# Cross-attention and mixture-of-experts kernel: the inverse sums of the softmax applied to the probabilities ahead of their transposes, by GpSimd and VectorE, in place of a transposed copy of them

## The chip, the core and the metric

The kernel runs on one core of one Trainium2 chip. A core has a matrix engine (TensorE, PE in the rows), which writes to eight banks of PSUM, and three engines for elementwise work: VectorE (DVE), ScalarE (ACT) and GpSimd (POOL). They share a memory of 128 partitions, SBUF. Each engine works off its own instructions in their order and waits for others on semaphores. The metric is the time of one execution on the device in microseconds (us); less is better.

## What is computed

32 sequences of 112 tokens with 512 channels go through one layer: causal cross-attention with 16 heads of 32 channels, then a mixture of eight experts and a shared expert. The change is in the attention.

```python
def _L0_xattn_ref(q, latent_kv, Wq, Wkv_expand, Wout):
    B, S, H, NH, L = (2, 512, 512, 16, 128)
    HD = H // NH
    qp = q @ Wq.T
    kv = latent_kv @ Wkv_expand.T
    k, v = jnp.split(kv, 2, axis=-1)
    ...
    scores = jnp.einsum('bhqd,bhkd->bhqk', qh, kh) * inv_sqrt_d
    scores = jnp.where(causal, scores, jnp.finfo(scores.dtype).min)
    attn = jax.nn.softmax(scores, axis=-1)
    out = jnp.einsum('bhqk,bhkd->bhqd', attn, vh)
    out = out.transpose(0, 2, 1, 3).reshape(b, sq, H)
    return out @ Wout.T

x = x + _L0_xattn_ref(_layernorm(x, axis=-1), ctx_512, L0_xattn_Wq, L0_xattn_Wkv_expand, L0_xattn_Wout)
x = x + _L0_ffn_ref(_layernorm(x, axis=-1), ...)
```

## The kernel before, in words

The program has three phases: attention and routing (phase A), the experts (63 tiles of 128 tokens), and the shared expert with the sum of all. Phase A runs over eight groups g of four batches j, so batch t is 4g + j; two further rounds of the loop drain the pipeline and begin the shared expert (`hidden0`, `project0`). One round for one batch is a *step*. All order is written by hand: each engine has a function for its step, and the engines meet on semaphores. The four upper PSUM banks are handed round by the table `TURNS`; the four lower ones hold the scores.

**TensorE's step t** (`step`, then `next_front`): value product of batch t (L823), mask (L937) and scores (L947) of batch t; 16 transposes of the *probabilities of batch t-1* (L956), four to a bank; four transposes of `rinv_wide` (L964); the products of probabilities and values, `outT`, of batch t-1 (L975); transposes of a normalised row block (L984, `normT`, batch t-3); output projection of batch t-2 (L823, `proj`); router (L1013); in the third step of a group two rank products (L914, L915); queries and keys of the next batches (L823). Large products are made of three, from a high and a low part of each operand (`_hi`, `_lo`).

**ScalarE's step**: `v_sb`; four copies `probsT` of the transposed probabilities out of PSUM (L1240); 16 exponentials of batch t with their row sums `rsum` (L1251), and after the eighth of them the copy `rinvT` (L1229); after the sixteenth `aT_hi` (L1262); then queries, keys and the next input's high part. `exp_done` counts halves of eight heads.

**VectorE's step**: `rinv` = 1/`rsum` of batch t-1 (L1685); twice the maximum over half of the scores and `minus_max` (L1692, L1694); statistics of the next input (L1580, L1583); `xn2T` (L1650); the low part of an input (L1605); `attnT` = `outT` times `rinvT` (L1717); `x1`, the residual sum of batch t-2 (L1726); `logits`; statistics of `x1`; `aT_lo` (L1738); and then `choices`: in the groups from the third on (g = 2 to 6) a chain of small instructions that chooses experts for the group before, 10 in the first step (j = 0), 11 lines in the second (13 instructions) and 6 in the fourth (`place`; not in g = 6). The third step has three others (`route_z`). In g = 7 the choices stand behind `minus_max`.

**GpSimd's step**: `rinv_wide` (L1486), `rinv` of batch t-1 copied 32 times for each head; indirect DMAs of token lists (L1439, two a step); in the first and the third step of a group the split of the context (L1430, L1432); `scaled_root` (L1419, L1421); `rows` for batch t-2: twice a small instruction and `xn` (L1474), which `normT` of the next step waits for. In g = 7 and later `rows` stands ahead of the indirect DMAs.

The whole scores bank of batch t may be written only when batch t-1's exponentials are done (L937 waits for `exp_done`).

## Time and profile before

| | us |
|---|---|
| median of 3 runs | 1514.03 (1512.74 to 1515.2) |
| the profiled execution, its own time | 1509.76 |
| span of its profile | 1508.0 |
| PE busy in the span | 1482.2 (98%) |
| DVE, ACT, POOL busy | 857.5, 653.0, 592.4 |
| granted TensorE clock | 0.999 of full speed |

A profile page first gives the busy time of each engine over the whole span, then the span in 40 slices of 37.7 us with a digit for the busy tenths of each, then the chain of work that ended last. Phase A fills the first eleven slices or so. Timelines list instructions in order of time, with an idle time and who ended it in brackets; the chain of waits lists at each moment what the end of the kernel hung on.

### The profile page before, as it was taken

The page shows a single profiled execution, that of the slowest core. Times are in us where ns is not written, and L with a number is a line of the kernel's source. Part 1 is how long each engine was busy: PE and PEld are TensorE (multiplying, and loading weights), DVE is VectorE, ACT ScalarE, POOL GpSimd, SP SyncE. Part 2 cuts the span into 40 slices and gives each one's busy share as a digit, 9 for nine tenths or more (in the row PEclk, how much of TensorE's full clock was granted, in tenths as well). Part 3 has the DMA queues.
Part 4 walks back from the last instruction along what each step waited for, and adds up shares of the span by engine and source line. Part 5 has one row for each costly group of instructions (what it writes and reads, how often), then busy time and mean ns, then how long its engine had stood idle before and what let it go on. Part 6 is the DMA issues. An engine that isn't in the chain of part 4 may idle for free.

```text
span 1508.0 us, 28385 instructions
## 1 busy us (share of the span) xinstructions
PE 1482.2 (98%) x10074; PEld 1261.6 (84%) x10074; DVE 857.5 (57%) x1458; ACT 653.0 (43%) x1836; POOL 592.4 (39%) x505
## 2 busy tenths in 40 slices
PE   8999999999989999999999999999999999999999
PEld 7788888888778899999999999887888888888887
DVE  5566777777756587786877867455223232223322
ACT  6999998999843322332332333332112121211211
POOL 3333455555552387595775864102101102011010
PEclk9999999999999999999999999999999999999999
DMA  6244434434365689877868765553303122030110
GB/s 225 87 118 118 118 112 117 117 95 121 82 139 111 179 309 340 275 246 264 284 232 275 279 215 175 176 202 88 95 15 112 28 73 61 6 112 28 59 54 28
DMA packets 102905, 217.44 MB, mean 144 GB/s; under 512 B 43696, under 2 KB 48816, under 8 KB 98064
## 3 DMA queue, kind: packets, MB, share of 16 engines
q1 hardware_dynamic: 91184, 184.71, 37.8%
q0 software_dynamic: 11616, 31.35, 7.2%
q8 instruction: 63, 1.03, 0.3%
q14 instruction: 42, 0.34, 0.1%
HBM read 168.86 MB, written 47.17 MB: 143 GB/s over the span
## 4 chain that ended last, share of the span: by engine, by line
PE 86%; ACT 7%; DVE 3%; issue 3%; POOL 1%; DMA 0%; DVEq 0%; POOLq 0%; ACTq 0%
PE psum L823 61%; PE psum L1146 11%; ACT probs L1251 5%; PE psum L956 2%; PE psum L906 2%; PE psum L1048 2%; PE psum L947 2%; PE psum L1072 1%; PE psum L975 1%; PE psum L1013 1%; ACT probsT L1240 1%; PE psum L964 1%; PE psum L984 1%; PE psum L937 1%; PE psum L837 0%
## 5 line engine op out<-in xcount | busy, mean ns | idle before, releaser
L1568 POOL DMA_INDIRECT routed<-expert_out_dram,slot_b x56 | 56.7, 1012 | 478.5 <-DVE slot_b L2016 328.0
L1251 ACT ACTIVATE probs<-psum,minus_max,rs 112x112 f32<-112x112 f32 x512 | 222.2, 503 | 3.6 <-DVE minus_max L1694 3.4
L2034 DVE TENSOR_TENSOR h_s<-psum,silu_s 128x512 f32<-128x512 f32 x66 | 45.7, 692 | 298.3 <-PE psum L823 290.0
L823 PE MATMUL psum<-nT_hi,ws_hi 128*128 128x512 f32 x528 | 208.8, 395 | 3.4 <-DVE nT_lo L1957 3.1
L823 PE MATMUL psum<-nT_lo,ws_hi 128*128 128x512 f32 x528 | 208.6, 395 | 0.0
L823 PE MATMUL psum<-nT_hi,ws_lo 128*128 128x512 f32 x528 | 208.6, 395 | 0.0
L1540 POOL DMA_INDIRECT xg<-normed_dram,tile_ids x63 | 149.9, 2380 | 36.1 <-DMA tile_ids<-lists_dram 17.4
L823 PE MATMUL psum<-wj_hi,gT_hi 128*128 128x352 f32 x504 | 162.8, 323 | 0.0
L823 PE MATMUL psum<-wj_hi,gT_lo 128*128 128x352 f32 x504 | 162.3, 322 | 0.0
L823 PE MATMUL psum<-wj_lo,gT_hi 128*128 128x352 f32 x504 | 161.8, 321 | 0.0
L1371 ACT ACTIVATE silu_s<-psum 128x512 f32<-128x512 f32 x66 | 39.4, 597 | 242.9 <-PE psum L823 242.9
L1251 ACT ACTIVATION_READ_ACCUMULATOR probs<-psum,minus_max,rs 112x1 f32 x512 | 135.7, 265 | 0.0
L1374 ACT ACTIVATE hs_hi<-h_s 128x512 fp32r<-128x512 f32 x66 | 41.7, 632 | 199.0 <-DVE h_s L2034 196.0
L1942 DVE TENSOR_TENSOR wj_lo<-wj_raw,wj_hi 128x2816 fp32r<-128x2816 f32 x35 | 121.7, 3476 | 9.4 <-POOL wj_hi L1523 7.2
L823 PEld LDWEIGHTS psum<-nT_hi,ws_hi 128*128 128x128 f32 x528 | 99.2, 188 | 27.6 <-DVE nT_lo L1957 3.5
L1523 POOL TENSOR_SCALAR wj_hi<-wj_raw 128x2816 fp32r<-128x2816 f32 x34 | 87.4, 2570 | 83.1 <-issue 75.8
L823 PEld LDWEIGHTS psum<-nT_hi,ws_lo 128*128 128x128 f32 x528 | 99.2, 188 | 23.8
L823 PEld LDWEIGHTS psum<-nT_lo,ws_hi 128*128 128x128 f32 x528 | 99.2, 188 | 23.3
L1146 PE MATMUL psum<-ws_lo,hs_hi 128*128 128x512 f32 x264 | 103.4, 392 | 0.0
L1146 PE MATMUL psum<-ws_hi,hs_hi 128*128 128x512 f32 x264 | 103.3, 391 | 0.0
L1146 PE MATMUL psum<-ws_hi,hs_lo 128*128 128x512 f32 x264 | 102.9, 390 | 0.0
L823 PEld LDWEIGHTS psum<-wj_lo,gT_hi 128*128 128x128 f32 x504 | 94.9, 188 | 2.6
(256 smaller groups left out, 3446.2 us busy)
## 6 DMA issues: line engine op xcount, KB each, us to landing
wj_raw<-in_w_experts SPq DMA_DIRECT2D x35, 1408.0 KB
wj_raw<-in_w_experts SPq DMA_DIRECT2D x35, 768.0 KB
wj_raw<-in_w_shared SPq DMA_DIRECT2D x22, 768.0 KB, 4.4
expert_out_dram<-y_c SPq DMA_DIRECT2D x63, 256.0 KB
base<-x_dram SPq DMA_DIRECT2D x8, 1024.0 KB, 5.9
xT_raw<-in_xT SPq DMA_DIRECT2D x32, 224.0 KB
x_in<-in_x SPq DMA_DIRECT2D x32, 224.0 KB
x_res<-in_x SPq DMA_DIRECT2D x32, 224.0 KB, 3.1
```

Of the source, the lines that this page charges most:

```text
L823: mm = pe.matmul(out_ap, u, v, start=(n == 0), stop=(n == last))
L906: mm = pe.matmul(bank(j), u, v, start=(c == 0 and q == 0), stop=(c == SC - 1 and q == 2))
L947: mm = pe.matmul(psum[0:SEQ, r, m * SEQ:(m + 1) * SEQ], qT[g % 2][rows, m, tok], kT[rows, m, tok], start=False, stop=(m == KC - 1))
L1146: mm = pe.matmul(bank(j), u, v, start=(i == 0 and q == 0), stop=(i == SC - 1 and q == 2))
L1251: done = act.activation(probs[:, j % 2, 4 * r + m, :], psum[0:SEQ, r, m * SEQ:(m + 1) * SEQ], ACT.Exp, bias=minus_max[:, r, m:m + 1], scal ...
L1371: act.activation(silu_s[:, :], bank(b), ACT.Silu).then_inc(emptied_b[b], 1)
L1374: act.activation(hs_hi[:, i % 2, :], h_s[:, :], ACT.Copy).then_inc(S["hs_hi_made"], 1)
L1523: pool.tensor_scalar(wj_hi[b][:, FC_COLS], wj_raws[b][:, FC_COLS], 1.0, 0.0, ALU.mult, ALU.add).then_inc(S["wc_hi_made"], 1)
L1540: pool.indirect_dma_start(out=xg[b][:, :], out_offset=None, in_=normed_dram, in_offset=bass.IndirectOffsetOnAxis(ap=tile_ids[:, k % ROUND: ...
L1568: pool.indirect_dma_start(out=routed[:, b % 2, c, :], out_offset=None, in_=expert_out_dram, in_offset=bass.IndirectOffsetOnAxis(ap=slot_b[ ...
L1942: dve.tensor_tensor(wj_lo[b][:, FC_COLS], wj_raws[b][:, FC_COLS], wj_hi[b][:, FC_COLS].bitcast(F32), ALU.subtract).then_inc(S["wc_split"], 1)
L2034: dve.tensor_tensor(h_s[:, :], bank(b), silu_s[:, :], ALU.mult).then_inc(emptied_b[b], 1)
```

## The change

The probabilities are multiplied by the inverse sums before they are transposed. GpSimd multiplies heads 0 to 7 of a batch in place as soon as their eight exponentials are done, VectorE heads 8 to 15 when all are. With that `rinv_wide`, its transposes, the copy `rinvT` and the product `attnT` go; `aT_hi` and `aT_lo` are made directly from the bank of `outT`, and ScalarE makes `aT_hi` after the fourth exponential. The order of the sums follows that of the probabilities. The freed SBUF goes into a gap, so that what follows keeps its place.

```diff
@@ TURNS
-    TURNS += [((_j, "sumT", 0), 1, 5), ((_j, "outT", 0), 1, 7),
+    TURNS += [((_j, "outT", 0), 1, 7),
@@ TensorE, step
-                    pe.wait_ge(S["exp_done"], 2 * t)
+                    pe.wait_ge(S["first_normed"], t)
+                    pe.wait_ge(S["normed"], t)
                     for i in range(4):
                         b = take(g, j, "probsT", i)
...
-                if there(g, j, 1):
-
-                    pe.wait_ge(S["rinv_spread"], t)
-                    b = take(g, j, "sumT")
-                    for m in range(KC):
-                        mm = pe.transpose(psum[:, b, m * SEQ:(m + 1) * SEQ], rinv_wide[:, 4 * m:4 * m + 4, :].rearrange("s h d -> s (h d)"),
-                                          ident[0:SEQ, 0:SEQ])
-                    mm.then_inc(filled[b], 1)
...
-                        pe.wait_ge(S["attnT_split"], t - 1)
+                        wait_emptied(pe, g, j - 1, "outT")
@@ ScalarE, body
+                    def attnT_high():
+                        if there(g, j, 3):
+                            wait_filled(act, g, j - 1, "proj")
+                        b = turns.bank("outT")
+                        wait_filled(act, g, j, "outT")
+                        act.activation(aT_hi[:, (j + 1) % 2, :, :].rearrange("p k s -> p (k s)"), bank(b, P, GT), ACT.Copy).then_inc(S["attnT_hi_made"], 1)
...
-                                                          accum_out=rsum[:, j % 2, 4 * m + r:4 * m + r + 1])
+                                                          accum_out=rsum[:, j % 2, 4 * r + m:4 * r + m + 1])
+                                if r == 0 and there(g, j, 1):
+                                    attnT_high()
                             done.then_inc(S["exp_done"], 1)
-                            if i == 0 and there(g, j, 1):
-                                rinv_to_rows()
@@ GpSimd, body
-                        pool.wait_ge(S["rinv_made"], t)
-                        settled(pool)
-                        pool.tensor_copy(rinv_wide[:, :, :], rinv[:, :].unsqueeze(2).to_broadcast([SEQ, HEADS, HD])).then_inc(S["rinv_spread"], 1)
...
                     if there(g, j, -1):
                         scaled_root(t + 1)
+                    if there(g, j, 0):
+                        pool.wait_ge(S["rinv_made"], 2 * t + 1)
+                        settled(pool)
+                        pool.tensor_tensor(probs[:, j % 2, 0:8, :], probs[:, j % 2, 0:8, :], rinv[:, 0:8].unsqueeze(2).to_broadcast([SEQ, HEADS // 2, SEQ]),
+                                           ALU.mult).then_inc(S["first_normed"], 1)
@@ VectorE
+            def normalise(t, i):
+                half, n = slice(8 * i, 8 * i + 8), 2 * t + i
+                dve.wait_ge(S["exp_done"], n + 1)
+                at_least(dve, S["normed"], t)
+                at_least(dve, S["first_normed"], t)
+                dve.reciprocal(rinv[:, half], rsum[:, t % 2, half]).then_inc(S["rinv_made"], 1)
+                if i == 0:
+                    return
+                dve.wait_ge(S["rinv_made"], n + 1)
+                dve.tensor_tensor(probs[:, t % 2, half, :], probs[:, t % 2, half, :], rinv[:, half].unsqueeze(2).to_broadcast([SEQ, HEADS // 2, SEQ]),
+                                  ALU.mult).then_inc(S["normed"], 1)
...
                 if there(g, j, 1):
-                    dve.reciprocal(rinv[:, :], rsum[:, (j + 1) % 2, :]).then_inc(S["rinv_made"], 1)
+                    normalise(t - 1, 1)
...
                     b = turns.bank("outT")
-                    dve.tensor_tensor(attnT[:, :], bank(b, P, GT), rinvT[:, :], ALU.mult).then_inc(emptied[b], 1)
+                    dve.wait_ge(S["attnT_hi_made"], t)
+                    hi = aT_hi[:, (j + 1) % 2, :, :].rearrange("p k s -> p (k s)")
+                    dve.tensor_tensor(aT_lo[:, (j + 1) % 2, :, :].rearrange("p k s -> p (k s)"), bank(b, P, GT),
+                                      hi.bitcast(F32), ALU.subtract).then_inc(emptied[b], 1)
...
-                if there(g, j, 1):
-
-                    dve.wait_ge(S["attnT_hi_made"], t)
...
+                if there(g, j, 0):
+                    normalise(t, 0)
                 if is_late(g, 0) or not is_late(g, 2) or (j < TB - 1 and not is_late(g)):
                     choices(g, j)
```

VectorE, end of a fourth step (j = 3) and begin of the next, before. `rt_eq` to `slots_i` are the six instructions of `place`, `rinv` to `minus_max` the next step's head:

```order
L1583 BN_AGGR mv<-stat 112x2
L1738 TENSOR_TENSOR aT_lo<-attnT,aT_hi 128x448
L1815 TENSOR_TENSOR rt_eq<-rt_rank,rt_one 112x32
L1816 TENSOR_REDUCE route<-rt_eq 112x4
L1817 CAST slots_i<-route 112x4
L1815 TENSOR_TENSOR rt_eq<-rt_rank,rt_one 112x32
L1816 TENSOR_REDUCE route<-rt_eq 112x4
L1817 CAST slots_i<-route 112x4
L1685 RECIPROCAL rinv<-rsum 112x16
L1692 TENSOR_REDUCE smax<-psum 112x8
```

The same place in the changed program:

```order
L1566 BN_AGGR mv<-stat 112x2
L1666 RECIPROCAL rinv<-rsum 112x8
L1802 TENSOR_TENSOR rt_eq<-rt_rank,rt_one 112x32
L1803 TENSOR_REDUCE route<-rt_eq 112x4
L1804 CAST slots_i<-route 112x4
L1802 TENSOR_TENSOR rt_eq<-rt_rank,rt_one 112x32
L1803 TENSOR_REDUCE route<-rt_eq 112x4
L1804 CAST slots_i<-route 112x4
L1666 RECIPROCAL rinv<-rsum 112x8
L1670 TENSOR_TENSOR probs<-probs,rinv 112x896
L1683 TENSOR_REDUCE smax<-psum 112x8
```

A first reciprocal now stands ahead of the choices, `aT_lo` has gone to the front of the step, and the multiplication of eight heads stands between the choices and the next maximum.

GpSimd, from `rows` of a fourth step to `scaled_root` in the next, before (`rs` and `xn` are `rows`, the last two `rs` are `scaled_root`):

```order
L1474 TENSOR_SCALAR xn<-x,mv,rs 112x512
L1486 COPY rinv_wide<-rinv 112x512
L1439 DMA lists_dram<-token_id,slots_i 28672x1 x2
L1419 TENSOR_SCALAR rs<-mv 112x1
L1421 TENSOR_TENSOR rs<-rs,neg_half 112x1
L1419 TENSOR_SCALAR rs<-mv 112x1
L1421 TENSOR_TENSOR rs<-rs,neg_half 112x1
```

and in the changed program:

```order
L1458 TENSOR_SCALAR xn<-x,mv,rs 112x512
L1423 DMA lists_dram<-token_id,slots_i 28672x1 x2
L1403 TENSOR_SCALAR rs<-mv 112x1
L1405 TENSOR_TENSOR rs<-rs,neg_half 112x1
L1483 TENSOR_TENSOR probs<-probs,rinv 112x896
L1403 TENSOR_SCALAR rs<-mv 112x1
L1405 TENSOR_TENSOR rs<-rs,neg_half 112x1
```

The copy at the head of the step is gone, and a multiplication of 896 columns stands between `scaled_root` and `rows`.

## Rows read from the trace of the kernel before

**Rows 1.** The page: busy time by engine, and ScalarE's busy tenths in 40 slices.
```profile
PE 1482.2 (98%) x10074; PEld 1261.6 (84%) x10074; DVE 857.5 (57%) x1458; ACT 653.0 (43%) x1836; POOL 592.4 (39%) x505
...
ACT  6999998999843322332332333332112121211211
```
**Rows 2.** Chain of waits, batch 7 of phase A: start us, us, engine and line.
```profile
110.31 1.68 PE psum L956 x16
...
111.99 0.57 PE psum L964 x4
...
116.78 0.70 PE psum L1013 x8
...
122.70 0.34 PE psum L956 x2
```
**Rows 3.** The same chain: the transposes L956 at the heads of groups 6 and 7.
```profile
326.44 1.68 PE psum L956 x16
...
377.84 0.54 PE psum L956 x4
```
**Rows 4.** Timeline of ScalarE, batch 7: start us, us, line, out<-in, shape, count.
```profile
110.87 1.84 ACT L1240 ACTIVATE probsT<-psum 112x448 f32<-112x448 f32 x4 [1.01 <-PE psum L956]
...
119.74 0.70 ACT L1262 ACTIVATE aT_hi<-attnT 128x448 fp32r<-128x448 f32 x1
```
**Rows 5.** Timeline of VectorE, batch 7.
```profile
117.19 0.68 DVE L1726 TENSOR_TENSOR x<-psum,x_res 112x512 f32<-112x512 f32 x1
...
118.76 0.18 DVE L1583 BATCH_NORM_AGGREGATE mv<-stat 112x2 f32<-112x6 f32 x1 [0.16 <-DVE stat L1580]
```
**Rows 6.** Timelines around a second step's choices: first, last, then VectorE's reciprocal and GpSimd's reply.
```profile
146.51 0.18 DVE L1798 SCALAR_TENSOR_TENSOR rt_rest<-rt_one,rt_p 112x32 f32<-112x32 f32 x1
...
149.09 0.17 DVE L1806 TENSOR_TENSOR chosen<-chosen,rt_pick 112x8 f32<-112x8 f32 x1
149.18 0.25 DVE L1685 RECIPROCAL rinv<-rsum 112x16 f32<-112x16 f32 x1
...
149.58 0.61 POOL L1486 COPY rinv_wide<-rinv 112x512 f32<-112x512 f32 x1 [2.15 <-issue]
```
**Rows 7.** Operands in SBUF alone: two by tile (ns min/median/max), one of a timeline.
```profile
L1459 POOL TENSOR_TENSOR n_lo<-xT_raw,n_hi x2: 1123/1123/1123, 9.8 to 10.9; 128x448 fp32r<-128x448 f32 x2
...
L1605 DVE TENSOR_TENSOR xT_lo<-xT_raw,xT_hi x16: 615/616/1082, 21.9 to 332.7; 128x448 fp32r<-128x448 f32 x16
...
13.12 1.22 DVE L1600 TENSOR_TENSOR wq_lo<-wj_raw,wq_hi 128x1024 fp32r<-128x1024 f32 x1 [1.13 <-ACT wq_hi L1169]
```
**Rows 8.** Timelines: VectorE and GpSimd at once, both reading SBUF, at three places.
```profile
543.46 2.92 POOL L1531 TENSOR_SCALAR wj_hi<-wj_raw 128x1536 fp32r<-128x1536 f32 x2
...
544.72 4.61 DVE L1942 TENSOR_TENSOR wj_lo<-wj_raw,wj_hi 128x2816 fp32r<-128x2816 f32 x1
...
23.92 0.92 POOL L1432 TENSOR_TENSOR ctx_lo<-ctx_in,ctx_hi 128x224 fp32r<-128x224 f32 x1
...
23.63 1.69 DVE L1605 TENSOR_TENSOR xT_lo<-xT_raw,xT_hi 128x448 fp32r<-128x448 f32 x2 [0.56 <-ACT xT_hi L1174]
...
145.35 2.08 POOL L1474 TENSOR_SCALAR xn<-x,mv,rs 112x512 f32<-112x512 f32 x1 [0.31 <-PE psum L823]
...
145.56 1.03 DVE L1738 TENSOR_TENSOR aT_lo<-attnT,aT_hi 128x448 fp32r<-128x448 f32 x1 [1.53 <-ACT aT_hi L1262]
```
**Rows 9.** Timelines: `place` and its cast beside `xn`.
```profile
222.17 2.08 POOL L1474 TENSOR_SCALAR xn<-x,mv,rs 112x512 f32<-112x512 f32 x1 [0.31 <-PE psum L823]
...
223.77 0.51 DVE L1817 CAST slots_i<-route 112x4 int32<-112x4 f32 x1
```
**Rows 10.** Chain of waits and timeline of TensorE: the transposes L956 of the last batches.
```profile
400.42 0.54 PE psum L956 x4
...
411.77 0.54 PE psum L956 x4
...
421.50 1.75 PE L956 MATMUL psum<-ident,probs 112*112 112x112 f32 x16 [1.53 <-ACT probs L1251]
```

36 lines of the change are left out of this document (5 added, 31 removed).

## The prediction

> **What bounds the kernel now.** I read the page first: PE is busy for 98% of the span, and ScalarE is dense only in the first eleven slices [rows 1], phase A, the one phase that the change touches. Then the chain of waits in a step of phase A without choices [rows 2]: it is all PE, and from one batch's transposes to the next takes 122.70 - 110.31 = 12.39 us. I call the start of these transposes R. In the groups with choices the chain leaves PE for VectorE and ScalarE; the mean group there takes (326.44 - 122.70) / 4 = 50.94 us [rows 2, 3], against 4 x 12.39 = 49.56 plus some 0.42 for the rank products. The last batches have no queries left and go at 411.77 - 400.42 = 11.35 [rows 10]. So the question is two-fold: how much shorter does PE's step get, and does anything new arrive later than PE at R?
>
> **PE's step.** The four transposes L964 go: 0.57 us on the chain [rows 2]. They also covered ScalarE's copies: these end at 110.87 + 1.84 = 112.71, R + 2.40 [rows 4]. `outT` would now start at R + 1.68 and reach the last quarter of its 32 products, after some 0.68, at R + 2.36: about 0.10 of waiting with the signal. PE's step becomes 12.39 - 0.57 + 0.10 = 11.92.
>
> **ScalarE.** `rinvT` goes and `aT_hi` takes its place, so the exponentials still end at 119.74, R + 9.43 [rows 4]. It gets 0.47 more idle time (the old `aT_hi`), which is worth nothing while PE is last.
>
> **VectorE until the first reciprocal.** `attnT` waited for `rinvT`; `aT_lo`, in its place, is done by some R + 5.3, ahead of `x1`, which now waits for PE's projection alone. That ended at 116.78, R + 6.47 [rows 2], now at R + 6.00, and with 0.15 for the signal `x1` starts at R + 6.15. From its start to the end of the statistics it is 118.94 - 117.19 = 1.75 [rows 5]: R + 7.90. The reciprocal of the first half ends at R + 8.10, and GpSimd answers a reciprocal after 149.58 - 149.43 = 0.15 [rows 6]: its multiplication starts at R + 8.25.
>
> **GpSimd's multiplication.** 448 columns of two SBUF operands took 1.12 us on GpSimd [rows 7], 224 took about 0.6 once let in [rows 8]; the slope is some 2.0 ns a column, so 896 take an estimated 2.03 us (bounds: twice 1.12 = 2.25; by `xn`, 2.08 for 512 columns, 3.64). It ends at R + 10.3; `rows` follows, 1.2 us of small work with its gaps and `xn` from about R + 11.5 to 13.6. `normT` needs it at R + 11.92 + 2.6: hidden, with 0.9 to spare. Indirect DMAs and `scaled_root` come after it and end some 6 us into the next step, ahead of the next reciprocal.
>
> **VectorE's multiplication.** 448 columns take 0.615, 1024 take 1.22 [rows 7]: 896 take about 1.09, and 0.2 for the reciprocal. In a step without choices it could start at R + 9.43 + 0.3 = 9.75 and end at 10.85, a full microsecond before PE wants it. But both engines would then read SBUF at once, which rows 8 show three times. `wj_lo` started while GpSimd worked until 543.46 + 2.92 = 546.38, and ended at 549.33, 2.95 later, its own whole length by the 1024-column row. The second of two `xT_lo` took 1.08 for 0.62 [rows 7] beside a `ctx_lo` of GpSimd, itself late by the first. Beside `xn`, whose 2.08 us outlast it, `aT_lo` took only 1.03: it was let in about 0.65 us after `xn` began. So a two-operand instruction of VectorE stands still while GpSimd reads; a GpSimd TENSOR_TENSOR reads to its end (one row of a short one), `xn` for 0.65 us. I take the first for the multiplication, since it is the same operation.
>
> The Trainium skill, in "SBUF — State Buffer", section "Who interferes with whom", calls this an exclusive lock: a VectorE instruction with two SBUF inputs and a GpSimd instruction that reads SBUF block each other for the whole instruction. The trace agrees for `wj_hi` and `ctx_lo`; `xn` was passed before its end. By the rule to the letter `xn` would also hold VectorE until R + 13.6, and the steps with choices would be some 1.5 us longer each than below; the rows decide against that.
>
> **Steps without choices.** VectorE's multiplication waits until R + 10.3, ends at 11.4, and with 0.1 for the signal is ready at 11.5. PE comes at 11.92. Hidden, by 0.4. Five such steps before R = 122.70: 5 x -0.47 = -2.35. The first three steps hang on ScalarE and on loads: 0.
>
> **Steps with choices.** Here the choices stand between the two reciprocals, in the middle of GpSimd's multiplication. They run at (149.26 - 146.51) / 13 = 0.21 each [rows 6].
> First step: two one-operand instructions until R + 8.5, then `rt_p` has two operands and waits until 10.3, ends 10.45; seven more, 1.5, and some 0.2 for `xn`'s reading: 12.2; reciprocal 12.4; multiplication 13.5 to 13.6; R' = 13.7.
> Second step: `rt_rest` slips in, `rt_eq` waits until 10.3; nine more, 2.1, and 0.3 for `xn`: 12.9; multiplication ends 14.2; R' = 14.3.
> Fourth step: the cast in `place` waits to the end of a GpSimd instruction even beside `xn`: 223.77 + 0.51 = 224.28, where `xn` ended at 224.25 [rows 9]. So it waits until 10.3; three more, 0.65; multiplication ends at 12.25; R' = 12.35.
> Third step: 11.92 + 0.42 for the ranks, and 0.06 if `rt_z` is caught: 12.4.
> Sum 52.75 against 50.94: +1.81 a group, four groups: +7.2. Group 6 has no `place`: 13.7 + 14.3 + 12.4 + 11.92 = 52.3 against 377.84 - 326.44 = 51.40: +0.9. Who waits in each case is PE, at the transposes; behind them all its work for the step. ScalarE waits in turn, and the maxima come after the multiplication but still 1 us ahead of ScalarE.
>
> **Last batches.** In group 7 the choices come early in the step and push `x1` to about R + 7.0, the first reciprocal to 8.95, GpSimd's multiplication to 9.1 to 11.1, just ahead of VectorE's (ready 9.75): that ends at 12.2, R' = 12.3 against 11.35, about +1.0, three times. Last batch: 421.50 - 411.77 = 9.73 from R to the last transposes [rows 10], which wait for nothing but exponentials; now 10.35 + 1.1 + 0.1 = 11.55, +1.8, less 0.8 for the L964 and its wait: +1.0. In the drain `aT_lo` leaves the stretch between statistics and choices: -0.5. Together +3.5.
>
> **Sum.** -2.35 + 7.2 + 0.9 + 3.5 = +9.25. The later phases are PE at full load behind phase A, and shift. The profiled execution took 1509.76, now 1519.0. It lies 4.3 under the median 1514.03; on the median's footing, which I forecast: 1523.3.
>
> **Rivals.**
> A short hold: the multiplication lets VectorE in after 0.65 us as `xn` does, or never stops it. Then the choices end at R + 10.6 to 11.2, R' is 12.0, 12.6, 12.34, 12.35: 49.3 a group, -1.65 x 4 = -6.6; group 6 -2.5; steps without choices -2.35; the last batches about 0: -11.4, time 1502.6. With no hold at all 48.2 to 48.5 a group and 1497. For it: `xn`, and that only one short row shows a TENSOR_TENSOR of GpSimd holding to its end. Against: `wj_hi` held for 2.6 us to its end. Chance 0.20.
> A slow multiplication: by `xn`'s rate 3.64 us, ending at R + 11.9. Then VectorE's multiplication ends at 13.0 even without choices, R' = 13.1, and every step with choices gains 1.6 more: 4 x 8.1 + 7 + 5 x 0.75 + 9.8 = +53, 1567. For it only that one of its operands is a repeated number; against: `rinv_wide` repeated the same one at 0.61 for 512 columns [rows 6]. It decides from 2.4 us on. Chance 0.05.
> Nothing in sum: VectorE wins the race at `rt_rest` and in group 7 in enough steps to bring +9 down to within 3. Chance 0.08, time about 1514.
> My forecast has 0.67, between 1515 and 1535: the 0.3 to 0.5 us by which the choices meet `xn`, or 0.2 more for the multiplication, move it by some 4 each.
>
> **How the numbers follow.** Range 1502 to 1535: the forecast with its bounds, the case of nothing, and the upper end of the short hold, about 0.82 together (0.64, 0.08 and half of the 0.20). A measurement tells 0.2%, 3 us, from no change. Slower: 0.67 + 0.05 = 0.72; within: 0.08; faster: 0.20.
>
> **What would show it.** R to R in a step without choices 11.9; first and second steps of a group 13.7 and 14.3 with PE idle before the transposes of the probabilities until VectorE's multiplication ends; `rt_p` in the first and the first `rt_eq` in the second step at some 1.8 us instead of 0.19; GpSimd's multiplication 2.0 us from R + 8.25. A short hold would show all choices at 0.2. Wrong would be the forecast if GpSimd came late to its multiplication, after VectorE's own, which would turn the waiting round.

## The result, and the profile of the changed kernel

| | before | changed |
|---|---|---|
| median | 1514.22 us (1512.74 to 1515.2, 4 runs) | 1523.13 us (1522.02 to 1524.24, 4 runs) |
| profiled execution, its span | 1509.76, 1508.0 | 1524.24, 1522.5 |
| granted clock, mean of that span | 0.999 | 0.992 |

The changed kernel is slower: ratio 1.007, with a 95% interval of 1.0057 to 1.0082 (the two medians alone give 1.006). The forecast was 1523.3.

The page of the changed kernel answers to [rows 1]. PE's work has shrunk by 2.8 us and VectorE's has grown by 40, GpSimd's by 44; the matrix engine is busy for 97% of a longer span.

```profile
PE 1479.4 (97%) x9946; PEld 1253.0 (82%) x9946; DVE 897.5 (59%) x1490; ACT 639.4 (42%) x1804; POOL 636.0 (42%) x505
```

As in the prediction, R is the start of the transposes of the probabilities (L954 now). I read the first of each batch from TensorE's timeline, for every kernel in the same way, and take the differences of four places: R(8), the begin of the groups with choices; R(28), their end; R(32), the last batch; and the span. The tables below use these columns.

| | R(8) | R(8) to R(28) | R(28) to R(32) | behind R(32) | span |
|---|---|---|---|---|---|
| before | 122.6 | 255.1 | 43.7 | 1086.5 | 1508.0 |
| changed | 120.6 | 264.4 | 50.1 | 1087.5 | 1522.5 |
| difference | -2.1 | +9.3 | +6.3 | +1.0 | +14.5 |

The program of the phases behind phase A is unchanged; what the +1.0 behind R(32) is made of stands in the part on the prediction. First the chain of waits in a step without choices, which answers to [rows 2]: start us, us, engine and line.

```profile
108.53 1.68 PE psum L954 x16
110.20 0.75 PE psum L965 x24
...
110.99 0.40 PE psum L965 x8
...
120.62 0.43 PE psum L954 x3
```

The L964 are gone, and the step takes 12.09 where it took 12.39. The product `outT` (L965) starts at once and stops after 24 of its 32 parts, because ScalarE's last copy of `probsT` is not there.

Then the first step with choices. The timeline of VectorE (start us, us, line, operation, out<-in, idle before) and below it GpSimd's and TensorE's of the same stretch; compare [rows 6]:

```profile
129.18 1.61 DVE L1769 TENSOR_TENSOR rt_p<-rt_e,rt_r 112x32 f32<-112x32 f32 x1
...
132.15 0.66 DVE L1782 TENSOR_TENSOR rt_one<-prefer,route 112x32 f32<-112x32 f32 x1
132.84 0.20 DVE L1666 RECIPROCAL rinv<-rsum 112x8 f32<-112x8 f32 x1
133.07 1.09 DVE L1670 TENSOR_TENSOR probs<-probs,rinv 112x896 f32<-112x896 f32 x1
...
129.07 1.69 POOL L1483 TENSOR_TENSOR probs<-probs,rinv 112x896 f32<-112x896 f32 x1 [3.74 <-DVE rinv L1666]
...
132.00 2.08 POOL L1458 TENSOR_SCALAR xn<-x,mv,rs 112x512 f32<-112x512 f32 x1 [0.31 <-POOL rs L1405]
...
134.27 1.72 PE L954 MATMUL psum<-ident,probs 112*112 112x112 f32 x16 [1.52 <-issue]
...
142.88 1.60 DVE L1779 TENSOR_TENSOR rt_eq<-rt_rest,route 112x32 f32<-112x32 f32 x1
...
142.75 1.68 POOL L1483 TENSOR_TENSOR probs<-probs,rinv 112x896 f32<-112x896 f32 x1 [4.11 <-DVE rinv L1666]
```

`rt_p`, an instruction of 32 columns, stands for 1.61 us, until 130.79, and GpSimd's multiplication ends at 130.76. Everything behind it is late: the choices, the second reciprocal, VectorE's multiplication, which ends at 134.16. TensorE has idled for 1.52 us and starts at 134.27. In the second step it is `rt_eq` that stands (1.60 us, beside the multiplication from 142.75, the last two lines). The steps of this first group take 13.7, 13.8, 12.5 and 12.6.

Last, the end of phase A, by windows of the span (us, busy us of each engine, PEclk, DMA share, GB/s) and in TensorE's timeline; before, the clock was 1.00 in all of it, and the transposes took 1.75 [rows 10]:

```profile
395.00:400.00 5.00, 5.00 (x89) 3.93 (x88) 4.08 (x4) 2.37 (x6) 4.22 (x4) 0.70 0.47 134
...
420.00:425.00 5.00, 3.56 (x48) 3.41 (x40) 4.77 (x8) 1.44 (x3) 4.37 (x4) 0.69 0.30 88
...
422.15 3.21 PE L954 MATMUL psum<-ident,probs 112*112 112x112 f32 x16 [1.44 <-issue]
...
435.04 3.21 PE L954 MATMUL psum<-ident,probs 112*112 112x112 f32 x16 [4.63 <-issue]
```

After idle times of 1.44 and 4.63 us the clock stands at its lower level, 1.2 GHz, and the same 16 transposes take 3.21 us.

### The profile page after: what moved, and what is told of

Read it like the earlier page. It is cut to its first block, busy times and chain, and to the rows that moved or that the text cites. A ratio compares the mean times of both kernels' runs of the same rounds, so it can differ in the third digit from the quotient of the medians.

```text
span 1522.5 us, 28070 instructions
## 1 busy us (share of the span) xinstructions
PE 1479.4 (97%) x9946; PEld 1253.0 (82%) x9946; DVE 897.5 (59%) x1490; ACT 639.4 (42%) x1804; POOL 636.0 (42%) x505
## 4 chain that ended last, share of the span: by engine, by line
PE 91%; ACT 4%; issue 2%; DVE 2%; POOL 0%; DMA 0%; another core or an unknown queue 0%; POOLq 0%; DVEq 0%; ACTq 0%
PE psum L820 63%; PE psum L1136 11%; PE psum L954 3%; ACT probs L1241 3%; PE psum L944 2%; PE psum L903 2%; PE psum L965 2%; PE psum L1038 2%; PE psum L1062 1%; PE psum L1003 1%; PE psum L974 1%; PE psum L934 1%; ACT probsT L1230 1%; PE psum L834 0%; DMA routed<-expert_out_dram,slot_b 0%
## 5 line engine op out<-in xcount | busy, mean ns | idle before, releaser
L1523 POOL DMA_INDIRECT xg<-normed_dram,tile_ids x63 | 150.1, 2382 | 35.6 <-DMA tile_ids<-lists_dram 12.8
```

What stands on the lines that cost most here:

```text
L1523: pool.indirect_dma_start(out=xg[b][:, :], out_offset=None, in_=normed_dram, in_offset=bass.IndirectOffsetOnAxis(ap=tile_ids[:, k % ROUND: ...
```

## The experiments

My theory was the hold (H): VectorE's small instructions stand while GpSimd multiplies, and that pushes VectorE's own multiplication past the transposes. The rivals: that it is only the place and length of VectorE's new work (P), and that the loss is at the end, with the clock (C, K).

Each set of experiments ran beside the kernel before, whose median was 1512.59, 1512.07, 1512.32 and 1513.19 us there; the ratios below are against these. The changed kernel itself was not run again, so a difference from its 1523.13 is sure to some 2 us only.

### GpSimd multiplies one column

```diff
-    pool.tensor_tensor(probs[:, j % 2, 0:8, :], probs[:, j % 2, 0:8, :], rinv[:, 0:8]..., ALU.mult)
+    pool.tensor_tensor(probs[:, j % 2, 0, 0:1], probs[:, j % 2, 0, 0:1], rinv[:, 0:1], ALU.mult)
```

> The changed kernel, but GpSimd multiplies one column of the probabilities instead of 896: heads 0 to 7 are left without their inverse sums. Everything else, the waits and signals too, is unchanged. Theory H (hold): VectorE's instructions with two SBUF operands, and its cast, stand still while GpSimd's multiplication reads, and that is what pushes VectorE's own multiplication past the transposes. Then rt_p in a group's first step and the first rt_eq in its second go back from 1.6 us to 0.19; the choices end at some R + 10.6 (one of them beside xn, +0.5), R to R' in the first step is 12.2 instead of 13.65 and in the second 12.8 instead of 13.8, the fourth 12.1; a group takes 49.6 instead of 52.9, five of them -16, and the last batches give back 1 to 3: 1504 to 1507. Rival P (place): what costs is only that a reciprocal and a multiplication of 1.09 us stand behind the choices; then the group keeps 52 to 53 us and the time stays within 3 of the changed kernel's 1523. Rival C (the end): the loss is the clock and the drain at the last batches; then the groups keep their 52.9 and only the stretch behind R(28) gets shorter, by some 4: 1519.

Measured 1511.15 (1506.05 to 1514.73, 10 runs), 0.9992 of before (0.9979 to 1.0006). VectorE's timeline:

```profile
129.84 0.19 DVE L1769 TENSOR_TENSOR rt_p<-rt_e,rt_r 112x32 f32<-112x32 f32 x1
...
131.39 0.55 DVE L1782 TENSOR_TENSOR rt_one<-prefer,route 112x32 f32<-112x32 f32 x1
```

| | R(8) | R(8) to R(28) | R(28) to R(32) | span |
|---|---|---|---|---|
| one column | 121.2 | 248.9 | 50.9 | 1507.5 |

`rt_p` is back at 0.19, and five groups take 248.9 us, 15.5 less than in the changed kernel; 16 were expected. Against a run of the same 28 batches without the stands described in the last section (261.7 us, the kernel with neither multiplication in the last four batches, below) it is 12.8. Of the choices only the instruction beside `xn` is still long. P and C both fall for the groups: VectorE's multiplication is still there, and the groups gain. But the last four steps did not get shorter at all, where 1 to 3 were expected; so the time is 1511, not 1504 to 1507. One of these steps took 15.4, and in it ScalarE stood for 4.41 us, for which the trace names no releaser; GpSimd's indirect DMAs ran in the second half of it.

### GpSimd writes zeros instead

```diff
-    pool.tensor_tensor(probs..., ALU.mult).then_inc(S["first_normed"], 1)
+    pool.memset(gap_a[0:SEQ, 0:1664], 0.0).then_inc(S["first_normed"], 1)
```

> The changed kernel, but GpSimd writes 1664 columns of a spare tile with zeros (448 columns took it 0.46 us, so about 1.7) in the place and with the waits and signals of its multiplication: it is as long busy, but reads no SBUF. Heads 0 to 7 are left without their inverse sums. Theory H in its form 'it is GpSimd's reading': VectorE goes through, rt_p 0.19, the same time as with the multiplication of one column, 1504 to 1507, except that rows and xn come 1.7 later and xn holds one instruction, as in the changed kernel. Rival W: any work of GpSimd on SBUF, writing too, holds VectorE's two-operand instructions; then rt_p still takes 1.6, a group 52.9, the time 1523. Rival P as before: 1523 without a long rt_p.

Measured 1513.58 (1511.54 to 1516.71, 10 runs), 1.0007 of before (0.9998 to 1.0017). VectorE's timeline and GpSimd's:

```profile
129.32 0.19 DVE L1768 TENSOR_TENSOR rt_p<-rt_e,rt_r 112x32 f32<-112x32 f32 x1
129.54 1.15 DVE L1769 TENSOR_SCALAR rt_g<-rt_ge 112x4 f32<-112x4 f32 x1
...
129.18 1.49 POOL L1483 MEMSET gap_a<- 112x1664 f32 x1 [3.24 <-DVE rinv L1665]
```

Neither form of the expectation holds as it stood. `rt_p`, with two operands, passes beside the write; the next instruction, `rt_g`, with one operand and a number, stands until the write's end (129.54 + 1.15 = 130.69, against 129.18 + 1.49 = 130.67). So the hold is not GpSimd's reading alone: writing holds another kind of VectorE's instructions. A first step takes 13.0 here and a second 12.2 to 12.7, since the second's choices have a copy, but no such instruction, within the 1.5 us. Five groups took 252.7: reading costs 11.7 us more than writing for about as long.

### VectorE multiplies all heads

```diff
-                if i == 0:
-                    return
...
-                    if there(g, j, 0):
-                        pool.wait_ge(S["rinv_made"], 2 * t + 1)
-                        settled(pool)
-                        pool.tensor_tensor(probs..., ALU.mult).then_inc(S["first_normed"], 1)
```

> The changed kernel, but VectorE multiplies heads 0 to 7 too, right behind its first reciprocal, and GpSimd none. Nothing is left out. That puts 1.09 us on VectorE ahead of the choices in place of GpSimd's 1.69 beside them. Theory H: VectorE is through at R + 9.3, the choices (2.1 and 2.7 us, +0.5 beside xn) end at 11.5 to 12, the second multiplication at 12.9 and 13.4: R to R' 12.9 and 13.5 in the first two steps, 12.5 and 12.1 in the others, a group 51.1 instead of 52.9, so -1.8 x 5 = -9, and 1513 to 1517. Rival P: what costs is VectorE's own work on the path; doing more of it there adds 1.09 to each of the first two steps: 15 us a group is 55, the time 1533.

Measured 1516.76 (1514.76 to 1518.31, 7 runs), 1.0028 of before (1.0015 to 1.004); R(8) to R(28) 259.0, R(28) to R(32) 49.7. First steps 13.4, second 13.65. Without any help of GpSimd the kernel is some 5 to 6 us faster than with it: 1.09 us on VectorE ahead of the choices costs less than 1.69 us of GpSimd beside them. P, which asked for 1533, falls. The first steps are 0.5 longer than I expected: the choices of the first step took 2.6 with their gaps and `xn`, not 2.1.

### The choices behind VectorE's multiplication

```diff
                 if there(g, j, 1):
                     normalise(t - 1, 1)
+                if j in (1, 2) and not is_late(g):
+                    choices(g, j - 1)
```

> The changed kernel, but the choices of a group's first and second step stand a little later on VectorE: behind the next step's second reciprocal and multiplication, ahead of its maxima. Nothing is left out, GpSimd's multiplication is as long as before. Theory H: VectorE's multiplication is then ready at R + 9.75, waits for GpSimd until some R + 10.2 and ends at 11.3, ahead of PE as in the steps without choices; the choices run from 11.3 to 13.4 and 14.0, with nothing to hold them; the first maximum ends at R' + 2.4 and 3.0 against ScalarE's copies at R' + 2.4. R to R' is 12.1 and 12.1 to 12.6; a group 49.0 to 49.6 instead of 52.9, -3.5 x 5 = -17: 1504 to 1507, under the kernel before. Rival P' (it is the length of the choices wherever they stand, since maxima, exponentials and PE form one ring): a group stays above 51.5, the time above 1516. In either case the fourth step keeps its 12.5.

Measured 1515.51 (1511.19 to 1519.93, 10 runs), 1.0018 of before (1.0004 to 1.0031); R(8) to R(28) 260.3. The steps of the first group: 12.1, 12.1, 15.2, 12.6. The first two are what H said, and the hold is gone from them. The third is what neither theory had. TensorE's timeline there, and a window of 5 us:

```profile
151.88 0.86 PE L1003 MATMUL psum<-gates_sb,xn2T 128*112 128x9 f32 x8 [0.77 <-DVE xn2T L1633]
...
155.66 0.57 PE L820 MATMUL psum<-xT_hi,wq_hi 128*128 128x448 f32 x1
...
155.00:160.00 5.00, 5.00 (x63) 4.14 (x61) 1.37 (x3) 3.35 (x11) 4.52 (x4) 0.71 0.83 229
```

The second step's 2.7 us of choices, ahead of the maxima, made `xn2T` late. The router waited 0.77 us for it, and in the work behind that idle time the clock fell: the query products, 0.36 each at first, took 0.57. So 2.7 us were lost where one copy was 0.8 late. The five third steps tell the two parts apart: the router waited 0.77, 0.30, 0.95, 0.40 and 1.22 us in them; they took 15.2, 13.3, 15.5, 13.4 and 15.5, and the clock fell in the first, third and fifth only. Some 2 us of each long one are the clock. In sum a group takes 52.1 us, above the 51.5 that P' asked for, but not for its reason, since the first steps all took 12.1. K was not on the list for this run, and should have been.

### The first reciprocal earlier

```diff
                     dve.tensor_tensor(x1[:, j % 2, :], bank(b, SEQ), x_res[:, j % 2, :], ALU.add).then_inc(emptied[b], 1)
+                if there(g, j, 0):
+                    normalise(t, 0)
...
-                if there(g, j, 0):
-                    normalise(t, 0)
```

> The changed kernel, but VectorE takes the first reciprocal right behind the residual sum x1, ahead of logits and of the statistics, so some 1.1 us earlier; GpSimd's multiplication starts at R + 7.3 instead of 8.4 and ends at R + 9.0 instead of 10.1. Nothing is left out. Theory H (hold): VectorE's choices begin at R + 8.2 as before but are held only until 9.0, 0.4 us instead of 1.4; R to R' in the first two steps of a group 12.5 and 13.0 instead of 13.7 and 13.8, a group 50.3 instead of 52.9, -13 in five groups, 1509 to 1511. Rival P (length and place of VectorE's work alone): the same instructions stand ahead of the second multiplication, a group stays above 52 and the time within 3 of 1523. That rival has fallen for GpSimd's part with the multiplication of one column (a group 49.2); here it could come back only if xn, now earlier too, holds as much.

Measured 1508.13 (1506.06 to 1511.29, 10 runs), 0.998 of before (0.997 to 0.9989), 13 to 15 us under the changed kernel. R(8) to R(28) 251.7, 50.3 a group as expected; R(28) to R(32) 47.8. VectorE's timeline and GpSimd's:

```profile
128.92 0.59 DVE L1769 TENSOR_TENSOR rt_p<-rt_e,rt_r 112x32 f32<-112x32 f32 x1
...
127.78 1.69 POOL L1483 TENSOR_TENSOR probs<-probs,rinv 112x896 f32<-112x896 f32 x1 [2.57 <-DVE rinv L1666]
```

No instruction was taken away or shortened; GpSimd only starts 1.2 us earlier, at R + 7.4 instead of 8.5, so that it is nearly done when the choices come. This is the strongest evidence for H, and the version, in which nothing is left out, beats both kernels. Not all of the 12.7 us in the groups is the hold: this run has none of the stands of the last section, which cost the changed kernel an estimated 2.7; the rest, 10.0, is the earlier start.

### One column each in the last four batches, and VectorE's alone

```diff
+                if t >= 28:
+                    dve.tensor_tensor(probs[:, t % 2, 8, 0:1], probs[:, t % 2, 8, 0:1], rinv[:, 8:9], ALU.mult)...
+                    return
```

and the same on GpSimd in the first of the two.

> The changed kernel, but for the last four batches (28 to 31) both engines multiply one column each: the probabilities of these batches are left without their inverse sums. It tells what the last four steps, 43.7 us before and 50.1 in the changed kernel, hang on; leaving out GpSimd's multiplication alone did not shorten them (50.9). Theory V: it is VectorE's own multiplication, 1.09 us in each of these short steps, and what it pushes; then R(28) to R(32) is 44 to 46 and the time 1517 to 1519. Rival K: it is the clock, which falls to half in these steps for a reason that lies in the order of the work (aT_lo and aT_hi at another place) and not in the multiplications; then it stays at 48 to 51 and the time at 1522 to 1524.

> The changed kernel, but VectorE multiplies one column only for the last four batches (28 to 31), GpSimd all of its own: heads 8 to 15 of these batches are left without their inverse sums. With neither multiplication the last four steps took 43.9 us, with both 50.1, with VectorE's alone 50.9 in a run in which ScalarE stood still for 4.4. Theory V (VectorE's 1.09 us in each of these steps, and the clock that falls behind its wait): R(28) to R(32) is 44.5 to 46.5, the granted clock 1.0 there. Rival G (GpSimd's multiplication is what comes last in them): 48 to 50.

| | R(28) to R(32) | time (runs) |
|---|---|---|
| both multiply | 50.1 | 1523.13 (4) |
| VectorE alone (first experiment) | 50.9, of it 4.4 ScalarE's stand | 1511.15 (10) |
| GpSimd alone | 48.9 | 1522.3 (1517.63 to 1525.64, 5) |
| neither | 43.9 | 1517.41 (1512.76 to 1521.82, 10) |

With neither, the last four steps take what they took before, 43.7. So the multiplications are what lengthens them, and not the new place of `aT_hi` and `aT_lo`. This rests on the one execution that was profiled, a fast one (1512.87, mean clock 0.998); six of the ten took 1517.3 to 1521.8 at a lower mean clock, and where they lost it was not looked at. The second run was to find which: V said 44.5 to 46.5 without VectorE's, G 48 to 50 without it, and it took 48.9. V falls; yet the first experiment has, by estimate, about 46.5 with VectorE's alone (50.9 less ScalarE's 4.4), so that neither engine's is the one cause. In the profile of the kernel with neither, the clock is 1.00 in every window of 5 us up to 425, and 0.68 at 425 to 430, where TensorE had idled for 3.37 us ahead of R(32); with GpSimd's it is 0.66 at 395 to 400 and 0.53 at 435 to 440:

```profile
395.00:400.00 5.00, 5.00 (x67) 3.65 (x67) 2.25 (x3) 2.40 (x8) 4.22 (x5) 0.66 0.88 150
...
435.00:440.00 5.00, 5.00 (x49) 4.34 (x50) 0.86 (x5) 2.29 (x5) 3.67 (x5) 0.53 0.22 50
```

How much of the 6 us is the clock and how much the steps' own length was not separated.

### The choices in four pieces

```diff
                 if j == 0 and routes(g):
                     choose(g - 1, 0)
+                    if is_late(g, 0):
+                        choose(g - 1, 1)
                 if j == 1 and routes(g):
-                    choose(g - 1, 1)
+                    choose(g - 1, 2)
+                    if is_late(g, 0):
+                        choose(g - 1, 3)
...
                 if there(g, j, 1):
                     normalise(t - 1, 1)
+                if j in (1, 2) and routes(g) and not is_late(g, 0):
+                    choose(g - 1, 2 * j - 1)
```

with the reciprocal behind `x1` as in "The first reciprocal earlier". `choose(n, c)` is now one of four pieces c, of 5, 5, 6 and 6 instructions; the second step's choices are 12 in the traces and the code, 22 with the first's, and the texts on record count one too many.

> The changed kernel with the first reciprocal behind x1, and with the 23 instructions of the choices cut in four: five at the end of a group's first step, five behind the second multiplication at the begin of its second step, six at the end of that, seven behind the multiplication at the begin of the third. Group 7 has the same places instead of behind its maxima. Nothing is left out. Theory H: a piece at the end of a step runs from R + 8.2, is held until 9.0 and ends by 10.1; the second multiplication ends at 11.3 to 11.5, ahead of PE; a piece at the begin delays xn2T by 1.1 to 1.5 us, to R + 5.2, ahead of the end of PE's projection at 6.0, so that the clock does not fall as it did with all of the second step's choices there. All steps 12.1, the third 12.5: a group 48.9, -20 in five groups, the last batches 48 instead of 50: 1500 to 1503, below both kernels. Rival K (the clock): any choices ahead of the maxima leave PE short of work, it halves its clock as in the run before, a group stays above 50.5 and the time above 1510.

> The kernel before, with the same four pieces of the choices at the same places (behind the reciprocal where the changed kernel has the multiplication), group 7 too. Nothing is left out. It tells whether the spreading helps by itself. Theory H: there was no hold to be avoided, and choices cost it only what a group has over four plain steps, 50.9 - 49.98 = 0.9; -5 in five groups, 1508 to 1510, so that the changed kernel with the same order stays 6 to 9 ahead of it. Rival S (the gain is all from the spreading): it falls by as much as the changed kernel does, to 1500 to 1503.

| | R(8) | R(8) to R(28) | R(28) to R(32) | time | ratio to before |
|---|---|---|---|---|---|
| changed, four pieces | 121.0 | 245.9 | 46.7 | 1501.59 (1500.64 to 1503.62, 4 runs) | 0.9936 (0.9919 to 0.9952) |
| before, four pieces | 123.5 | 257.8 | 46.8 | 1518.54 (1518.08 to 1519.67, 4 runs) | 1.0046 (1.003 to 1.0063) |

The changed kernel with its work in another order is the fastest of all, 10.5 us under the kernel before and some 20 under the changed one, at the time that H gave; K, which asked for more than 1510, falls. The steps of its first group take 12.1, 12.1, 12.5 and 12.7. VectorE's timeline: the piece at the end of a step, then the multiplication, then the next piece, and it is TensorE that comes last, without idle time.

```profile
129.45 0.58 DVE L1774 TENSOR_TENSOR rt_p<-rt_e,rt_r 112x32 f32<-112x32 f32 x1
...
130.27 0.18 DVE L1776 RECIPROCAL route<-rt_g 112x4 f32<-112x4 f32 x1
130.78 0.20 DVE L1670 RECIPROCAL rinv<-rsum 112x8 f32<-112x8 f32 x1 [0.33 <-ACT probs L1241]
131.02 1.09 DVE L1674 TENSOR_TENSOR probs<-probs,rinv 112x896 f32<-112x896 f32 x1
132.03 0.18 DVE L1795 TENSOR_REDUCE route<-rt_p 112x4 f32<-112x32 f32 x1
...
133.03 1.17 PE L954 MATMUL psum<-ident,probs 112*112 112x112 f32 x10
```

The control missed its expectation by 9 us, on the bad side. The first, second and fourth steps went to 12.4 as expected, the third to 14.5. Its bank 7 passes from `outT` to the rank products, and in the kernel before it is VectorE's `attnT` that empties it, which the pieces made late:

```profile
157.16 0.35 PE L914 MATMUL psum<-rt_pick,before_f 112*112 112x32 f32 x2 [1.07 <-DVE attnT L1723]
```

So both theories on it fall, and the order of pieces is not a gain by itself. That it fits the changed kernel because there VectorE waits between `outT` and `aT_lo` for one copy only is argued, not tested. An order made for the kernel before might do better than this one; that was not tried.

### GpSimd multiplies twice

```diff
+    pool.tensor_tensor(gap_a[0:SEQ, 0:896]..., probs[:, j % 2, 0:8, :], rinv[:, 0:8]..., ALU.mult)
     pool.tensor_tensor(probs[:, j % 2, 0:8, :], probs[:, j % 2, 0:8, :], rinv[:, 0:8]..., ALU.mult)
```

> The changed kernel, but GpSimd does its multiplication twice, first into a spare tile and then in place: it reads SBUF for 3.4 us instead of 1.69, the case that the prediction called the slow multiplication. Nothing is left out. Theory H (hold): it ends at R + 11.9 instead of 10.1, so that in the first two steps of a group the held instruction grows from 1.6 to 3.3 us and R to R' from 13.7 to 15.4; in the steps without choices VectorE's own multiplication is held to R + 11.9 and ends at 13.0, R to R' 13.1 instead of 12.1; a group 15.4 + 15.4 + 13.4 + 13.9 = 58.1 instead of 52.9. So +26 in five groups, +5 in the first steps, +6 at the end: 1560. Rival W (the hold is a part of the time only, what costs is the multiplication's start): the steps grow by less than half of the 1.69, 1535 or less.

Measured 1575.31 (1573.8 to 1577.45, 4 runs), 1.0422 of before (1.0402 to 1.0443). VectorE's timeline and GpSimd's in a first step:

```profile
136.85 1.62 DVE L1771 TENSOR_TENSOR rt_p<-rt_e,rt_r 112x32 f32<-112x32 f32 x1
138.50 1.58 DVE L1772 TENSOR_SCALAR rt_g<-rt_ge 112x4 f32<-112x4 f32 x1
...
136.73 1.69 POOL L1483 TENSOR_TENSOR gap_a<-probs,rinv 112x896 f32<-112x896 f32 x1 [3.34 <-DVE rinv L1668]
138.38 1.68 POOL L1485 TENSOR_TENSOR probs<-probs,rinv 112x896 f32<-112x896 f32 x1
```

Each multiplication holds one instruction to its own end: `rt_p` gets in between the two, and `rt_g` is held by the second. The first group's first step is 15.3 (expected 15.4; all five 14.9 to 16.1), steps without choices are 12.8 to 13.2 (13.1). W falls. Second, third and fourth steps are up to 1.4 longer than expected, and the clock fell in nine stretches between R(8) and R(28), which the expectation had not; together that makes 1575 of 1560. In the steps without choices the order of the two turns round: VectorE's multiplication gets in between GpSimd's two, and GpSimd's second one stands, 2.53 us long from 98.84, so that TensorE waits for GpSimd:

```profile
101.42 1.75 PE L954 MATMUL psum<-ident,probs 112*112 112x112 f32 x16 [0.52 <-POOL probs L1485]
```

### The reciprocal ahead of x1, and the lists later

```diff
+                if there(g, j, 0):
+                    normalise(t, 0)
                 if there(g, j, 2):
                     dve.wait_ge(xres_loaded[j % 2], 16 * (2 * g + j // 2))
```

> The kernel with the first reciprocal early and the choices in four pieces, but the reciprocal ahead of x1 instead of behind it: GpSimd may start at R + 6.3 to 6.9 instead of 7.4. Nothing is left out. Theory H: the piece of choices from R + 8.2 on is no longer held at all (0.4 us in the run before), but no step hangs on it any more, so the steps of the groups keep 12.1; in the last batches, where x1 came as late as R + 8.3 behind a slow clock, GpSimd is done earlier, and R(28) to R(32) falls from 46.7 to some 45.5: 1499 to 1501 against 1501.6. Rival X: the reciprocal waits for the eighth exponential at R + 6.2 to 6.9 and holds up x1, which PE's projection bank and the statistics hang on; then the steps with choices go to 12.3 to 12.6 and the time to 1503 to 1508.

Measured 1526.69 (1525.03 to 1527.42, 5 runs), 1.0092 of before (1.0076 to 1.0108): 25 us more than with the reciprocal behind `x1`, against all expectation. The first group's steps are 12.1, 12.1, 12.5, 12.1. Then it goes wrong in another place. TensorE, VectorE, ScalarE and GpSimd at R(12):

```profile
169.46 1.75 PE L954 MATMUL psum<-ident,probs 112*112 112x112 f32 x16
...
171.34 1.09 DVE L1689 TENSOR_REDUCE smax<-psum 112x8 f32<-112x896 f32 x1 [2.66 <-remote]
...
172.01 1.84 ACT L1230 ACTIVATE probsT<-psum 112x448 f32<-112x448 f32 x4 [2.90 <-remote]
...
169.23 1.09 POOL L1423 DMA_INDIRECT lists_dram<-token_id,slots_i  x1 [0.17 <-issue]
```

In a step without choices the maximum starts at R + 0.21 and the copy at R + 0.63; here they come at R + 1.88 and R + 2.55. That happens in ten steps (the expectation below says eleven, a miscount; in two of the ten the copy comes at R + 1.9), and in each of the ten GpSimd's first indirect DMA starts 0.16 to 0.39 us ahead of R; where it starts at R + 0.1 or later, the maximum comes at R + 0.2 to 0.3 (up to R(28)). X, an `x1` held up, is not seen. The next run moves the DMAs:

```diff
-                        scatter(g - 2, ITEMS[2 * j:2 * j + 2])
...
                     if there(g, j, -1):
                         scaled_root(t + 1)
+                        scatter(g - 2, ITEMS[2 * j:2 * j + 2])
```

> The kernel with the reciprocal ahead of x1 took 1526.7 instead of the 1500 expected: in 11 of its steps VectorE's first maximum comes 1.9 to 2.5 us behind R instead of 0.2 to 0.3, ScalarE's first copy 2.4 to 2.7 behind it instead of 0.63, and in each of these, and in no other of them, GpSimd's first indirect DMA (two of 1.06 and 0.94 us) starts 0.16 to 0.39 us ahead of R. This kernel is that one with the two indirect DMAs behind scaled_root, which ends at some R + 5: they start at R + 5 and end at 7.2, so that the multiplication comes at R + 7.3 instead of 6.7. Nothing is left out. Theory D (the indirect DMAs, started just ahead of the transposes, keep VectorE and ScalarE from answering TensorE): the late maxima are gone in all steps, steps are 12.1 and 12.5 again, a group 48.9, the time 1499 to 1503. Rival X (it is the early reciprocal, or the transfers that this order brings together): they stay in as many steps wherever the indirect DMAs are, the time above 1515.

Measured 1526.57 (1522.92 to 1529.26, 5 runs), 1.0094 of before (1.0077 to 1.0111). From R(9) to R(28) no maximum comes at R + 1.9 or later any more, which is D's first half. The time did not fall, because the move made a new wait: `place` may not write `slots_i` anew before the lists' DMAs have read it, and in the fourth steps it now stands for them.

```profile
271.19 0.27 DVE L1808 TENSOR_TENSOR rt_eq<-rt_rank,rt_one 112x32 f32<-112x32 f32 x1 [4.23 <-DMA lists_dram<-token_id,slots_i]
```

Behind it stands the second multiplication, and TensorE idled 3.67 us. So D is supported by one coincidence ten times over and by its absence here, not by a time. Why two engines should not answer for 2 us while GpSimd issues an indirect DMA stays open, and the DMA's time alone does not decide it: in the changed kernel it starts 0.1 us ahead of R several times, and there, where VectorE's maximum was already running, ScalarE's copy was on time. In the kernel with four pieces it starts 0.20 us ahead of R(26), at 341.57; ScalarE stood waiting, and was on time at R + 0.63:

```profile
341.37 1.06 POOL L1423 DMA_INDIRECT lists_dram<-token_id,slots_i  x1 [0.18 <-issue]
...
342.20 1.85 ACT L1230 ACTIVATE probsT<-psum 112x448 f32<-112x448 f32 x4 [0.79 <-PE psum L954]
```

## Why the prediction was right, and where its sizes were off

The forecast of 1523.3 stands on a sum of +9.25, and the medians differ by 8.9. By the profiles alone, however, the sum would have been short: their spans differ by 14.5. Step by step:

**PE's step** was to shrink by 0.47 and shrank by 0.30. The L964 gave their 0.57 back; the wait for the last copy of `probsT` was mis-sized: `outT` takes from 110.20 to 111.39 in the chain above, 1.19 us, where its 32 parts took 0.90 in one piece in the same chain of before, so that its price is 0.29 and not 0.10. Up to R(8) it is -2.1 instead of -2.35, of which 0.9 came ahead of R(4). The line of the chain of before:

```profile
112.57 0.90 PE psum L975 x32
```

**GpSimd's multiplication** took 1.69 and not 2.03: a slope of 2.0 ns a column, taken from two full operands, was too steep for one with a repeated number. It started at R + 8.4 to 8.5 where I had 8.25, so its end, R + 10.2, was right to 0.1.

**The hold** was the step that decided, and it is shown: without GpSimd's multiplication the five groups are 15.5 us shorter, with its start 1.2 us earlier they are 12.7 shorter (12.8 and 10.0 against a run without stands), doubled it adds 1.6 to the first step. One reading in it was off: the prediction says that `wj_hi` held for 2.6 us, and its rows give 546.38 - 544.72 = 1.66, beside two of GpSimd's instructions and not one. The first step was 13.7 as forecast, the second 13.8 instead of 14.3 (GpSimd was done 0.1 earlier, and the nine instructions behind `rt_eq` took 2.1 us with `xn`'s share in it, where I had added 0.3 for that), the third 12.5, the fourth 12.6 in the first group and 13.0 in the next three instead of 12.35, and 13.1 in group 6 instead of 11.92. The cast stood there as forecast (1.57 and 1.54 us); but in groups 3 to 5, counted from g = 0, `xn2T` had stood for 1.5 us (see the last section), so that `x1`, the reciprocal and GpSimd were 0.4 later, and in group 6 TensorE waited 0.63 us for ScalarE's `kT`, behind such a stand before `aT_hi`. The groups: +9.3 instead of +8.1. The kernel with neither multiplication in the last four batches is the same program up to R(28), had no such stand, and took 261.7 us for the groups, +6.6, with fourth steps of 12.6 and 12.1: what was forecast is then 1.5 too much, and what came on top of it, some 2.7, was not forecast at all.

The Trainium skill, "SBUF — State Buffer", "Who interferes with whom", names the same lock. The runs agree for GpSimd's multiplication to its end (130.76 against `rt_p` until 130.79), and are milder for `xn`: `rt_one` was let in some 0.6 us after `xn` began (132.15 + 0.66 - 0.19 = 132.62, against 132.00), of its 2.08, as before the change.

**The last batches** were mis-sized most: +6.3 up to R(32) and +1.0 behind it instead of +3.5. The profile of before has a clock of 1.00 there, and I priced the steps at it; now it falls to the lower level three times, at 394 to 398, 422 to 425 and 432 to 438 us. The first three steps came to +3.2 together, where I had +3.0. The last one, 12.9 instead of 9.8, has the largest miss: its transposes took 3.21 us instead of 1.75, its exponentials and with them VectorE's multiplication came that much later, and so it is +3.1 instead of the +1.8 that I gave it. The second slow set, at R(32), falls into the drain; even so the experts' phase begins only 12.9 us later than before, after 13.5 at R(32), so that the drain gave back 0.6 (I had 1.3, the 0.8 and the 0.5). The remaining +1.5 arises far behind phase A. After a pause of 2.98 us that the kernel before has too (3.09), the clock fell in this execution and not in that of before:

```profile
1060.00:1065.00 5.00, 5.00 (x17) 3.92 (x16) 1.39 (x3) 0.60 (x1) 0.00 (x0) 0.66 0.51 190
```

I had no term for the clock at all.

**The footing.** I added 4.3 because the profiled run of before was under its median. The runs explain this gap: of 19 runs of the kernel before beside the second set of experiments, nine at a mean clock of 0.997 to 0.999 took 1509.0 to 1511.2, and ten at 0.993 to 0.995 took 1512.1 to 1514.4. Its profiled run was one without the fall, and the changed kernel's four runs were all at 0.992 to 0.994. So the missing clock term, by my estimate some 3 to 5 us, is in the profiles' difference and mostly not in the medians'. The forecast of the median was closer than its parts deserve: that the sum was 5.3 short by the profiles and the median came out within 0.2 is luck.

Of the rivals, the short hold is refuted by `rt_p`; the slow multiplication was the doubled run, whose mechanism is as described and whose 1575 lies near the 1567 worked out for it, though the clock has a part in it; "nothing in sum" did not occur.

## What to carry to other kernels

When work goes to an engine that shares a memory with another, ask what the other engine runs in those microseconds, and not only whether the path has room. Here the same two multiplications cost +9 us beside a chain of 22 small instructions and gain 10 us when the first starts 1 us earlier and the chain is cut in four: after a change is measured slower, look at the instructions that it stands beside before it is undone. A wait that is harmless in one version's order (a bank, a list's DMA) can be what ends the next, so each reordering needs its own profile.

## What the runs showed of the hardware that was not expected

Which instruction of VectorE is held depends on what GpSimd does. Beside a GpSimd multiplication that reads SBUF, those with two operands stood to its end (`rt_p` 1.61), and one with a single operand and a number too (`rt_g` 1.58); beside a write-only memset the former passed in 0.19 and the latter stood (1.15). A reduction passed beside the memset, and a reciprocal beside the multiplication (118.23, 0.20). And the hold goes both ways: GpSimd's second multiplication stood for 0.85 us beside VectorE's.

A short idle time of TensorE can cost more than itself: 0.77 us before the router were followed by a stretch at 0.71 and a step 2.7 us longer, while 1.37 to 1.62 us ahead of the transposes in the first steps of the changed kernel's groups were followed by none (clock 1.00 in every window of 5 us from 60 to 385). Runs of one kernel differ with it: with one column each in the last batches, four runs at a mean clock of 0.997 to 0.998 took 1512.8 to 1513.4, six at 0.989 to 0.995 took 1517.3 to 1521.8.

ScalarE and VectorE stood again and again without a releaser that the trace can name ("remote" in brackets), 0.4 to 4.4 us long, each time ahead of an instruction that reads what TensorE wrote: in all 7.5 us before `aT_hi` and 5.1 before `xn2T` in the changed kernel. One of these, 2.79 us in the drain, is on its chain. Their times are tied to GpSimd's indirect DMAs. GpSimd's two indirect DMAs and VectorE in a fourth step of the changed kernel:

```profile
215.35 1.06 POOL L1423 DMA_INDIRECT lists_dram<-token_id,slots_i  x1 [0.18 <-issue]
216.71 0.94 POOL L1423 DMA_INDIRECT lists_dram<-token_id,slots_i  x1 [0.31 <-issue]
...
218.36 0.62 DVE L1633 COPY xn2T<-psum 128x448 f32<-128x448 f32 x1 [1.52 <-remote]
```

The fourteen traces have 78 such stands of over 0.4 us in their first 500 us, none ahead of the first of these DMAs, and 77 of them end 0.4 to 1.1 us behind the end of one (the other is one of 2.65 us in the first experiment, and the 4.41 there began 2.6 us ahead of such a DMA). With two DMAs in a step of some 12 us, chance would put about one in eight there, by estimate. The late maxima of the run with the reciprocal ahead of `x1` are the same thing. Four kernels have none of them, the two fastest among them, and the kernel before has three; many waits beside such a DMA end on time, as the one at R(26) above. What decides it is open, and so is the cause.
